# The last batch of edges: three padding chunks fewer to gather, and another order of its left-over selection quads

## The reference

```python
h = (x @ W).reshape(N, HEADS, HEAD_DIM)
e = a_src[src] + a_dst[dst]; e = where(e > 0, e, NEG_SLOPE * e)
e_max = segment_max(e, dst); ex = exp(e - e_max[dst]); denom = segment_sum(ex, dst)
out = segment_sum(h[src] * (ex / (denom[dst] + 1e-16))[:, :, None], dst) + bias
...
msgs = z[dst] @ Wd + z[src] @ Ws + edge_weight * ww + bm
agg = segment_max(msgs, dst)
out = relu(z @ W1a + agg @ W1b + b1) @ W2 + b2
```

## Time and profile before

| | |
|---|---|
| median of 3 runs | 6849.09 us (6848.08 to 6849.81) |
| span of the profiled execution | 6856.8 us |
| busy: PE, ACT, POOL, DVE | 74%, 68%, 72%, 60% of the span |
| last gather of layer 0, layer 1 and layer 2 begins at | 2158.7, 4413.0 and 6709.4 us |

### The profile page before, as it was taken

One profiled execution on the slowest core, in us unless ns is written; L12 is line 12 of the kernel. 1 busy time (PEld: TensorE's weight loads), 2 busy tenths in 40 slices (PEclk: granted clock), 3 DMA queues, 4 the chain that ended last, 5 costly groups with the idle time before them and its releaser, 6 DMA issues.

```text
span 6856.8 us, 136148 instructions
## 1 busy us (share of the span) xinstructions
PE 5089.9 (74%) x24591; PEld 4780.1 (70%) x24591; DVE 4096.0 (60%) x11895; ACT 4663.9 (68%) x10649; POOL 4951.3 (72%) x5220
## 2 busy tenths in 40 slices
PE   7988888888887798888888888764555556556556
PEld 6987888888786797887888788654455445445455
DVE  3655555555556465555555555565666666666667
ACT  5877777777776687777777777774555555555558
POOL 5777777777774777777777777557777777777772
PEclk6555555555555655555555555567888788888879
DMA  8444444444443554444444444365655665565564
GB/s 232 128 119 117 115 122 119 116 119 120 118 114 72 152 130 115 117 121 119 114 121 119 117 117 121 82 185 151 177 166 163 177 172 164 168 178 167 162 183 137
DMA packets 820595, 943.49 MB, mean 138 GB/s; under 512 B 185720, under 2 KB 549570, under 8 KB 819522
## 3 DMA queue, kind: packets, MB, share of 16 engines
q1 hardware_dynamic: 658962, 595.34, 30.1%
q0 software_dynamic: 160256, 335.36, 21.4%
q10 hardware_dynamic: 432, 2.45, 0.1%
HBM read 883.19 MB, written 49.44 MB: 136 GB/s over the span
## 4 chain that ended last, share of the span: by engine, by line
PE 36%; POOL 22%; issue 14%; DVE 12%; DMA 11%; DVEq 2%; ACT 2%; SPq 1%; POOLq 0%; ACTq 0%
POOL G L682 22%; PE bA L780 13%; PE bS L815 12%; DVE acc L1415 4%; DMA G<-table,idx 4%; PE bM L815 3%; PE bE L815 3%; DMA st<-d_neg 3%; DVE bA L1644 2%; DMA G<-ztable,idx 2%; DVE ch L1650 1%; PE bA L703 1%; DVE G L1482 1%; PE bP L703 1%; DVEq L1281 1%
## 5 line engine op out<-in xcount | busy, mean ns | idle before, releaser
L682 POOL DMA_INDIRECT G<-table,idx x3328 | 3148.2, 946 | 1051.1 <-issue 921.8
L815 PE MATMUL bS<-G,S 128*128 x8816 | 2036.6, 391 | 362.2 <-DVE acc L1415 211.5
L815 PEld LDWEIGHTS bS<-G,S 128*128 128x128 f32 x8816 | 1753.4, 280 | 479.5 <-issue 471.4
L682 POOL DMA_INDIRECT G<-ztable,idx x1664 | 1573.8, 946 | 524.1 <-issue 467.5
L1068 ACT ACTIVATE S<-iota_row,nd 128x128 f32<-128x128 f32 x5904 | 1864.2, 387 | 69.1 <-issue 40.7
L780 PEld LDWEIGHTS bA<-adst,st 128*128 128x128 f32 x7872 | 1797.2, 333 | 126.2 <-issue 122.4
L780 PE MATMUL bA<-adst,st 128*128 x7872 | 1698.0, 340 | 91.2 <-issue 71.0
L1415 DVE TENSOR_TENSOR acc<-acc,bS 128x136 f32 (+1 forms) x4408 | 1277.0, 290 | 580.7 <-DVE acc L1415 94.6
L1072 ACT ACTIVATE S<-S,one_col 128x512 f32<-128x512 f32 x1476 | 1065.2, 722 | 56.5 <-issue 7.0
L1054 ACT ACTIVATE st<-xr,neg_p 128x512 f32<-128x512 f32 x984 | 699.8, 711 | 531.3 <-DMA xr<-d_drel 331.2
L703 PE MATMUL bA<-ident,G 128*128 128x128 f32 x1664 | 328.4, 339 | 704.6 <-DVE ch L1650 582.2
(11 more groups left out here) (217 smaller groups left out, 3988.3 us busy)
## 6 DMA issues: line engine op xcount, KB each, us to landing
xr<-d_drel SPq DMA_DIRECT2D x984, 256.0 KB
xr<-in_ew SPq DMA_DIRECT2D x312, 256.0 KB
st<-d_neg SPq DMA_DIRECT2D x312, 256.0 KB
G<-table,idx POOLq DMA_INDIRECT x3328
G<-ztable,idx POOLq DMA_INDIRECT x1664
isend<-in_ew SPq DMA_DIRECT2D x104, 256.0 KB
isend<-d_neg SPq DMA_DIRECT2D x104, 256.0 KB
table<-G SPq DMA_DIRECT2D x48, 264.0 KB, 4.9
```

Source lines behind the costliest of these rows:

```text
L682: pool.indirect_dma_start(G[:, r, c, 0:width], None, from_table, bass.IndirectOffsetOnAxis(ap=idx[:, r, c:c + 1], axis=0)).then_inc(gather ...
L815: mm = pe.matmul(bank_of(l, u, r, k)[:, j * w:(j + 1) * w], S[:, onehots(r, i), s, :], Gf[:, bass.ds(chunk_at[0][s], w)], start=True, stop ...
```

## The change

`LAST_C` is 29. For batch 51 (`ends`, or `chunks_of(b)`), in all three layers, POOL issues 29 gathers and not 32, and the counts that are waited for become smaller by the missing ones. `G` then holds in these three chunks what batch 46 left there; the targets of these chunks are padding.

In layers 0 and 1, for batch 51 alone, DVE does the left-over quads 4 and 5 (of batch 50) ahead of `logits`, quad 6 behind it, and none between `local_max`, `carry` and `segment_max`. PE does pairs 10 and 11 ahead of its wait for the logits. ACT does the new quads 1 and 2 ahead of `weights`.

```diff
+LAST_B = NB - 1
+LAST_C = -(-N_EDGES // P) - LAST_B * CB
...
+        def chunks_of(b):
+
+            return LAST_C if isinstance(b, int) and b == LAST_B else CB
+
+        def rows_landed(l, b, r, it):
+
+            short = 16 * (CB - LAST_C)
+            return 512 * landed(l, r, it) - short * ((l if r == LAST_B % RING else 0) + (1 if chunks_of(b) < CB else 0))
...
             def idx_load(l, b, r, it):
-                done = 512 * (landed(l, r, it) - 1)
+                done = rows_landed(l, None, r, it - 1)
...
-                    for c in range(CB):
+                    for c in range(chunks_of(b)):
...
-                    old(8, 10)
+                    ends = isinstance(b, int) and b == LAST_B
+                    old(8, 12 if ends else 10)
                     pe.wait_ge(e_made, l * NB + b + 1)
                     turn(ET, Ec).then_inc(e_turned, 1)
                     pe.wait_ge(a_read, l * NB + b + 1)
                     pe.nop(nofuse=True)
                     expand(0, 1)
-                    old(10, 12)
+                    if not ends:
+                        old(10, 12)
...
-                        pe.wait_ge(pieces[r][s // 2], 128 * (it + 1))
+                        short = CB - chunks_of(b) if s // 2 == 3 else 0
+                        pe.wait_ge(pieces[r][s // 2], 128 * (it + 1) - 16 * short)
...
-                    new(0)
+                    ends = isinstance(b, int) and b == LAST_B
+                    for i in range(3 if ends else 1):
+                        new(i)
                     weights(b, r)
...
-                dve.wait_ge(gathered[r], 512 * landed(l, r, it))
+                dve.wait_ge(gathered[r], rows_landed(l, b, r, it))
...
+                    ends = isinstance(b, int) and b == LAST_B
+                    if ends:
+                        old(4)
+                        old(5)
                     logits(b, r, it)
-                    old(4)
+                    old(6 if ends else 4)
                     local_max(b, r, it)
-                    old(5)
+                    if not ends:
+                        old(5)
                     carry(b, r)
-                    old(6)
+                    if not ends:
+                        old(6)
                     segment_max(b, r)
```

More of the change, by code:

```diff
@@ L1116, in body @@
                     expand(4, 5)
-                    new(0)
+                    ends = isinstance(b, int) and b == LAST_B
+                    for i in range(3 if ends else 1):
+                        new(i)
                     weights(b, r)
                     expand(5, 6)
-                    new(1)
+                    if not ends:
+                        new(1)
                     expand(6, 7)
-                    new(2)
+                    if not ends:
+                        new(2)
                     expand(7, 8)
```

## The result

The changed kernel takes 6833.11 us (median of 10 runs, 6830.68 to 6836.2), the one before 6849.77 us beside it (10 runs, 6848.08 to 6853.59): ratio 0.9975, 95% interval 0.9967 to 0.9983, that is 16.7 us. By the line of 13.7 us that the prediction drew between no change and faster, this is faster; the prediction had put 0.53 on no change and 0.45 on faster.

The account below looks back on a forecast made before the run. POOL's gathers were taken to bound each layer, leaving the last gathers and what follows to win: 3.7 + 1.9, 3.45 + 1.9 and 3.2 make 14.15, rounded to 14, so 6849.1 - 14 = 6835.1 us, range 6831.5 to 6839.5.

Parts of the forecast that it names:

- The gathers, layers 0 and 1: End of layers 0 and 1: three gathers fewer bring the logits forward 3.7 and 3.45 us, two quads mostly covered.
- The chain: Behind the logits, layers 0 and 1: new wait costs 2.23 us, two quad stretches go; 1.9 us won per layer.
- PE's clock: After PE's pause ahead of the logits: PE comes back at half clock, so the 1.43 us to DVE's start stand.
- rival (c): PE returns fast or the tail meets better clock moments: gain 15.5 to 17 us, time 6833; chance 0.12.
- ACT: Ahead of the exponentials: ACT waits 5 us for the exponents; its lead of two quads gives nothing.
- Layer 2: End of layer 2: the last gather starts 3.75 us earlier and DVE loses its whole pause, 3.2 us.
- The tails: From the exponents to the next layer's first gather: distance unchanged, the shift handed over whole.
- a growing stretch: Sign of being wrong: the stretches between the chain and the next layer's first gather grow.
- rival (b): A layer's tail might be 1.5 us longer and give part back: 11 us in all, time 6838; chance 0.13.
- (a): Behind the logits: the new wait shrinks the chain's 1.9 us to about 0.5; time 6837.7; chance 0.17.
- (d): ACT's exponentials, behind new quad 2, come late and stop the chain; 6851 us if 13 us late; chance 0.02.
- (e): Landing not tied to the last gather, only the order counts: about 4 us, time 6845; chance 0.02.

Follow-up runs that it names:

- one-quad kernel: Changed kernel, but DVE does quad 4 alone ahead of the logits, quad 5 behind, quad 6 between carry and segment maxima; PE makes their pairs earlier: 6829.17 us.
- fastest kernel: The changed kernel, with PE also doing quad 6's two pairs ahead of its wait for the logits in batch 51: 6824.94 us.

## Why the prediction was right, point by point

| stretch, us | before (2 profiles) | change (2 profiles) | my term | measured |
|---|---|---|---|---|
| last gather to logits, layer 0 | 4.46, 4.47 | 3.56, 4.23 | 3.7 with three gathers | 4.3 |
| the same, layer 1 | 4.45, 4.43 | 4.51, 3.31 | 3.45 | 4.3 |
| logits to exponentials, layer 0 | 13.36, 13.37 | 11.21, 11.20 | 1.9 | 2.2 |
| the same, layer 1 | 13.28, 13.30 | 11.20, 11.19 | 1.9 | 2.1 |
| exponentials to next gather, layer 0 | 156.5, 153.9 | 154.4, 154.0 | 0 | 1.0 |
| the same, layer 1 | 198.7, 200.0 | 200.9, 201.2 | 0 | -1.7 |
| last gather to end, layer 2 | 147.4, 147.0 | 147.7, 147.7 | 3.2 | 3.2 |

Each stretch is the difference of two starts in the timeline (the last row's ends at the end of the span); "measured" is the difference of the means, with 3.75 us added in the rows of the last gather, for three gathers. The sum is 15.4 us; the two comparisons of times gave 16.7 and 14.4 us. The range holds both, but 6833.11 us lies just outside the 6834 to 6837 us of the forecast itself, and the sum would be further from it without the tails, which take back 0.7 us that I had put at nothing.

**The gathers, layers 0 and 1.** Right in kind: the three gathers count in full. Two sizes were off. I kept the landing at 4.47 us; it is 3.35 to 3.42 us with 29 chunks, since the padding itself had made it late. And I took DVE's two quads as level with the landing, 0 to 0.3 us late; against the earlier landing they are up to 1.1 us late, and in one of four stretches not at all. The term came out at 4.3 us a layer in place of 3.7 and 3.45. In part this is luck. In all four stretches DVE decides, so the earlier landing only makes room, and the logits come 6.8 or 6.4 us after DVE starts quad 3 of batch 50. I took that start from one profile, 2.0 and 1.7 us ahead of the last gather that stays; from execution to execution, with the kernel before too, it lies 1.7 to 3.2 us ahead. With DVE where the first profile had it, the terms would be 3.4 and 3.5 us (an estimate from these numbers).

**The chain.** The new wait was well read. Counted from the logits' end, DVE starts quad 6 at +2.29 us where I had +2.37, and the scan of the local maxima at +4.18 where I had +4.33. So the wait costs 2.1 us and not 2.23; the pause of 2.27 to 2.29 us holds the 0.14 us that were there before. The two stretches went as read. My 0.2 us for bare hops was too much; 0.03 us shows between turn and scan. From the logits' end to the exponentials it is 10.37 us, a shade outside the 10.4 to 10.8 that I gave.

**PE's clock.** PE came back at 0.50 of full speed after a pause of 5.75 us, and the first pair took 1.30 us. The rule of the Trainium skill's page "TensorE: Matmul & The Clock Gate", part 1, held, and rival (c) didn't come true in this place. In layer 2 its mechanism did: in the first profile PE turns the last piece's rows in 0.63 us, at a granted clock of 1.00 over 6686 to 6688, where it took 1.09 us at 0.53 before. The measured 6833.11 us is rival (c)'s number, but most of (c)'s gain was to come from the wait behind the logits, and there PE was slow.

**ACT.** It waited 5.21 us for the exponents, as forecast (5), and in the one comparison, on the slower chip, its two quads ahead are worth nothing.

**Layer 2.** DVE's pause went, 3.2 us. That agrees, but DVE also came to this place 0.7 us earlier, counted from the last gather that stays, and a later pause took 0.5 us back; and the end of layer 2 spreads from 147.2 to 148.8 us over the other kernels with 29 chunks, so the term is good to a microsecond only.

**The tails.** Here the prediction did not hold: I had them rigid and at nothing, and had named a growing stretch as a sign of being wrong. Up to the third of the tail's quads they are rigid: the fourth starts 35.74 to 35.80 us after the exponentials in layer 0, in all ten profiles from chips of the first kind. Behind that they wander by 1 to 2.5 us. In layer 1 the four profiles with two quads ahead and 29 chunks have 200.9 to 201.7 us, all others from such chips, the one-quad kernel with 199.0 and the one with the new order and 32 chunks with 199.8 among them, 198.7 to 200.0. Whether the change itself costs 1.5 us there (rival (b) in small) or these are the wanderings, no run decides. On the slower chip the changed kernel has 199.0 and the one with ACT's old order 199.6, with two quads ahead and 29 chunks both, and the order of before 200.4, which speaks for the latter.

**The other rivals.** (a) is refuted by the chain itself, 2.1 to 2.2 us shorter in each layer where (a) had 0.5. (d): ACT was 5 us early, not late. (e) is refuted by the gathers alone, which give 11.7 us; the order alone gives 4.6.

## What to carry to other kernels

When work is moved into a pause, look at what is then first behind the pause and whether its input can be made earlier too: two more pairs ahead of PE's wait were worth another 4.3 us of chain here, since a ready quad had been the cover of PE's hop, and its successor was not ready. And ask whether the pause is there at all: on the slower chip DVE had none, and the same order cost it 2.4 to 2.7 us a layer. Padding that gathers is not free because its results aren't used; give it distinct sources, or leave it out. And before a profile's span is subtracted from another's, compare a step that should be the same in both.

## What the hardware showed that I had not expected

- Gathers whose 128 descriptors read one row land late: 4.45 us from the start of POOL's instruction to the logits with one row, 2.5 us with distinct rows, 3.4 us with 20 distinct ones and 108 of one row. In the first case the last gather is the third in a row of its kind. That distinct sources on top of the fastest kernel give a further gain was not tried; there DVE, not the landing, sets the logits.
- POOL's step from gather to gather was 1.2508 us in one execution and 1.2484 to 1.2491 us in all others on chips of that kind (layers 1 and 2): 11.1 us over a run.
- On one chip every kernel took 8500 us in place of 6850, with the chain behind the logits unchanged to a few hundredths (13.37 and 11.20 us) and the last gathers' copies through as early as elsewhere (3.0 us). DVE's logits came 18.0 to 22.9 us behind the last gather all the same, and ahead of none of its 104 logits does the changed kernel's trace there show DVE waiting for a gather, where it is 93 times and 535 us on a chip of the first kind. What slows the engines on that chip stays open.
